# Four reorderings in a ViT-layer kernel: reciprocal root, row normalisation, first low part, tail products

## The reference, cut to what matters

```python
pooled = x.reshape(Bb, Cc, n, K, n, K).sum(axis=(3, 5))      # K = 16, n = 14
h = jnp.einsum('bcij,ce->bije', pooled, channel_weights)     # 196 tokens of 192 for each image
h = h + attention(_layernorm(h))                             # 1 + qk + qk*qk/2, relu, divided by its sum
flat = _layernorm(h)
probs = softmax(flat @ router_w.T)                           # 8 experts
top_w, top_i = jax.lax.top_k(probs, 2)                       # weights normalised to their sum
for e in range(8):
    w_e = jnp.sum(top_w * (top_i == e), axis=-1)[:, None]
    out = out + w_e * (gelu(flat @ w1[e] + b1[e]) @ w2[e] + b2[e])
return h + out
```

## Time and profile before

| | |
|---|---|
| median of 3 runs | 1372.46 us (1367.8 to 1373.46) |
| profiled execution | 1380.3 us, span 1378.5 us |
| granted TensorE clock, mean | 0.939 |
| busy: PE / DVE / ACT / POOL | 1228.3 / 957.9 / 592.9 / 600.3 us |
| DMA | 284.42 MB, mean 206 GB/s |
| steps 0 to 3, alone | to 234 us |
| steps 4 to 15 with three tiles each | 234 to about 1080 us |
| four rounds of whole tiles, three of half tiles | to the end |

### The profile page before, as it was taken

The page is one execution under the profiler, slowest core; times in us unless marked ns, Lnnn a source line. Parts: engine busy times, 40 slices in busy tenths (PEclk is TensorE's granted clock), DMA queues, the critical chain, the costliest instruction groups (busy, mean ns, idle before and its releaser), DMA issues.

```text
span 1378.5 us, 26907 instructions
## 1 busy us (share of the span) xinstructions
PE 1228.3 (89%) x7299; PEld 1091.9 (79%) x7299; DVE 957.9 (69%) x3405; ACT 592.9 (43%) x1127; POOL 600.3 (44%) x485
## 2 busy tenths in 40 slices
PE   5867765999999899998989999999999989999996
PEld 3756654888888788887878888888888878898885
DVE  6799998787878687878777878787765433333453
ACT  1121222444445444544444444444354544444564
POOL 0103434335453545444546454535464554353433
PEclk9975557999999999999999999999999999999998
DMA  9779886778888778787787778787644555454554
GB/s 357 229 253 358 307 292 222 229 224 237 238 229 225 221 209 246 223 247 208 237 225 240 222 238 232 228 244 212 173 111 84 184 127 102 94 115 88 111 123 110
DMA packets 126552, 284.42 MB, mean 206 GB/s; under 512 B 24820, under 2 KB 70501, under 8 KB 126501
## 3 DMA queue, kind: packets, MB, share of 16 engines
q1 hardware_dynamic: 82762, 241.95, 54.0%
q0 software_dynamic: 43104, 41.25, 17.2%
q10 hardware_dynamic: 634, 0.61, 0.2%
HBM read 228.79 MB, written 54.95 MB: 206 GB/s over the span
## 4 chain that ended last, share of the span: by engine, by line
PE 44%; DVE 21%; DMA 11%; issue 11%; POOL 8%; ACT 5%; ACTq 0%; POOLq 0%; DVEq 0%
PE ps L997 15%; PE ps L966 14%; DVE red L1073 8%; DMA result<-ys,ridx 6%; POOL rows_d L608 5%; DMA rows_d<-rows,sloti 4%; PE ps L806 4%; POOL result L623 3%; DVE stats L1201 2%; PE ps L937 2%; PE ps L938 1%; ACT rows L720 1%; ACT hid L731 1%; DVE topi L1210 1%; PE ps L902 1%
## 5 line engine op out<-in xcount | busy, mean ns | idle before, releaser
L623 POOL DMA_INDIRECT result<-ys,ridx x210 | 334.2, 1591 | 325.8 <-issue 152.5
L997 PE MATMUL ps<-w2a,hid 128*128 x2520 | 456.3, 329 | 1.8 <-ACT hid L731 1.8
L997 PEld LDWEIGHTS ps<-w2a,hid 128*128 128x128 f32 x2520 | 419.5, 192 | 13.6 <-issue 2.6
L608 POOL DMA_INDIRECT rows_d<-rows,sloti x256 | 254.1, 993 | 400.3 <-DMA rows_d<-rows,sloti 146.8
L1073 DVE TENSOR_REDUCE red<-xbuf 128x21 f32<-128x672 f32 x448 | 360.0, 841 | 5.2 <-PE ps L870 2.4
L731 ACT ACTIVATE hid<-ps,b1s 128x512 f32<-128x512 f32 (+1 forms) x344 | 222.4, 653 | 229.8 <-PE ps L966 177.3
L966 PE MATMUL ps<-xh,w1h 128*128 128x512 f32 (+1 forms) x344 | 159.8, 465 | 45.5 <-ACT hid L731 32.2
L1333 DVE TENSOR_TENSOR w1l<-w1r,w1h 128x768 fp32r<-128x768 f32 x114 | 108.0, 952 | 81.6 <-ACT w1h L743 80.9
L966 PE MATMUL ps<-xb,w1h 128*128 128x512 f32 (+1 forms) x344 | 131.8, 383 | 0.0
L966 PE MATMUL ps<-xh,w1l 128*128 128x512 f32 (+1 forms) x344 | 131.5, 382 | 0.0
L966 PE MATMUL ps<-xb,w1l 128*128 128x512 f32 (+1 forms) x344 | 131.5, 382 | 0.0
(11 more groups left out here) (165 smaller groups left out, 1609.6 us busy)
## 6 DMA issues: line engine op xcount, KB each, us to landing
xbuf<-x SPq DMA_DIRECT2D x224, 672.0 KB, 5.9
w1r<-L_ffn_w SPq DMA_DIRECT2D x118, 384.0 KB, 4.6
xr<-rows_d SPq DMA_DIRECT2D x48, 402.0 KB, 3.7
result<-h1s SPq DMA_DIRECT2D x32, 294.0 KB
w2a<-L_ffn_w SPq DMA_DIRECT2D x8, 576.0 KB, 7.9
rows_d<-rows,sloti POOLq DMA_INDIRECT x256
rows_d<-pad SPq DMA_DIRECT2D x9, 402.0 KB, 4.6
result<-ys,ridx POOLq DMA_INDIRECT x210, 5.1
```

The costliest lines, as they stand in the source:

```text
L608: pool.indirect_dma_start(rows_d, bass.IndirectOffsetOnAxis(ap=sloti[:, k * NT + t:k * NT + t + 1], axis=0), rows[:, t, :], None).then_inc ...
L623: pool.indirect_dma_start(out, bass.IndirectOffsetOnAxis(ap=ridx[:, b, n:n + 1], axis=0), ys[:, b, n, :], None, compute_op=ALU.add).then_i ...
L997: last = mm(yout(g, b, n), hid[:, m % 3, cols], w, start=False, stop=m == MC - 1 and n % 2 == 1)
```

## The change

ORDER: R goes from the head of the third list to right behind S10 in the second, with it ahead of two names P and of Z1 on VectorE. In the third list V.0 goes from ahead of M1 to behind M2, and V.1 from ahead of M2 to behind W0. TensorE's and GpSimd's own order in ORDER stay as they are. LAST: G2 goes ahead of two names P. G1's Z goes from GpSimd to VectorE. TAIL_ORDER: N2 goes ahead of M5 in each tile; in the second list N3, N4 and N5 of the tile before go ahead of M0, M1 and M2, X0, N0, M3 and X1 go ahead of the row numbers and the row load (`<I B`), and W1 and Z1 behind M5.

```diff
--- before.py
+++ after.py
@@ -161,17 +161,17 @@
 ORDER = [
     """S1 M2 S2 P P L J P N0 N1 N2 X0 M3 W0 X1 S3 N3 P Z0 P P M4 S4 B P M5 W1 P P Z1 P P P Y N4 S5 N5""".split(),
     """M0 M1 M2 S6.0 P S6.1 N0 N1 X0 S6.2 P <I M3 X1 N2 P N3 W0 P S6.3 S7.0 <F <A S7.1 Z0 P P S8.0 L B M4 S8.1 P S8.2 M5 J P S8.3
-       S10 W1 P Z1 P""".split(),
-    """M0 R P <N4 <N5 <Y V.0 S11 M1 V.1 M2 S9 <I W0 V.2 N0 P X0 Z0 V.3 M3 N1 N2 P X1 W1 M4
+       S10 R P W1 Z1 P""".split(),
+    """M0 P <N4 <N5 <Y M1 M2 V.0 S11 S9 <I W0 V.1 V.2 N0 P X0 Z0 V.3 M3 N1 N2 P X1 W1 M4
        I P L B Z1 P P M5 <F Q0 Q1 Q2 Q3 <A""".split(),
     """M0 <Y <N3 <N4 <N5 <J M1 <F <A""".split(),
 ]
 LAST = """S3 P P P P P P P P P P S4 S5 P P P G0 G4 S6.0 S6.1 S6.2 S6.3 S7.0 P S7.1 P P G5 G1 P S8.0 S8.1 S8.2 S8.3 S10
-    R V.0 S11 V.1 V.2 S9 V.3 Q0 Q1 Q2 Q3 P P P P P G2 P P G3 P P P P""".split()
+    R V.0 S11 V.1 V.2 S9 V.3 Q0 Q1 Q2 Q3 P P P G2 P P P P G3 P P P P""".split()
 TAIL_ORDER = [
-    """L B J N0 M2 X0 W0 Z0 M3 X1 N1 M4 M5 W1 Z1""".split(),
-    """M0 M1 L J <N2 <Y M2 <N3 <N4 <N5 <I B N0 N1 X0 M3 X1 N2 M4 W0 Z0 W1 Z1 M5 I <F <A N3 N4 N5""".split(),
-    """M0 L B J <Y <F <A M1 M2 X0 W0 Z0 N0 M3 X1 N1 M4 M5 N2 F A N3 N4 I W1 Z1 N5 Y""".split(),
+    """L B J N0 M2 X0 W0 Z0 M3 X1 N1 M4 N2 M5 W1 Z1""".split(),
+    """<N3 M0 <N4 M1 L J <N5 <Y M2 X0 N0 M3 X1 <I B N1 M4 N2 W0 Z0 M5 W1 Z1 I <F <A N3 N4 N5""".split(),
+    """M0 L B J <Y <F <A M1 M2 X0 W0 Z0 N0 M3 X1 N1 M4 N2 M5 F A N3 N4 I W1 Z1 N5 Y""".split(),
     """M0 M1""".split(),
 ]
 PARTS = CHUNKS * HALVES
@@ -630,7 +630,7 @@
                     wait_first(pool, s_h, j * MC + m + 1)
 
             def Z(j, b, q):
-                if at_end[0] or b in LOW_BY_DVE:
+                if at_end[0] or b % 3 in LOW_BY_DVE:
                     return
                 nb = (b + 1) % 3
                 cols = slice(q * FF // 2, (q + 1) * FF // 2)
@@ -640,17 +640,13 @@
                 nc.gpsimd.tensor_tensor(w1l[:, :, cols], w1r[:, nb, q], w1h[:, :, cols].bitcast(F32),
                                         ALU.subtract).then_inc(s_w1l, 1)
 
-            def G1(s):
-                Z(-1, -1, 0)
-                Z(-1, -1, 1)
-
             wait_first(pool, d_pad, 32)
             for n in range(TP):
                 pool.indirect_dma_start(
                     out, bass.IndirectOffsetOnAxis(ap=padi[:, n:n + 1], axis=0),
                     pad[:, n, 0:E], None, compute_op=ALU.add).then_inc(d_add, 16)
 
-            schedule(pool, {"Q": Q, "H": H, "F": F, "A": A, "Z": Z, "G1": G1})
+            schedule(pool, {"Q": Q, "H": H, "F": F, "A": A, "Z": Z})
 
 
         @block.scalar
@@ -1323,7 +1319,7 @@
                                     xb[KB1:128, nb, 0:128 * g].bitcast(F32), ALU.subtract).then_inc(s_xd, 1)
 
             def Z(j, b, q):
-                if not at_end[0] and b not in LOW_BY_DVE:
+                if not at_end[0] and b % 3 not in LOW_BY_DVE:
                     return
                 nb = (b + 1) % 3
                 cols = slice(q * FF // 2, (q + 1) * FF // 2)
@@ -1344,6 +1340,10 @@
                 count_rows(1)
                 L(-2, -2)
                 L(-1, -1)
+
+            def G1(s):
+                Z(-1, -1, 0)
+                Z(-1, -1, 1)
 
             def G2(s):
                 now[:] = [0, -1]
@@ -1385,7 +1385,7 @@
                     P(s, p)
 
             schedule(dve, {"P": P_left, "S1": S1, "S2": S2, "T2": T2, "S6": S6, "S7": S7, "S8": S8, "S10": S10, "R": R,
-                           "S11": S11, "S9": S9, "L": L, "X": X, "I": I, "Z": Z, "G0": G0, "G2": G2},
+                           "S11": S11, "S9": S9, "L": L, "X": X, "I": I, "Z": Z, "G0": G0, "G1": G1, "G2": G2},
                      before_tail=list_ends)
     return nc
```

## The result

| | before | after |
|---|---|---|
| median | 1370.28 us (1367.8 to 1373.46, 4 runs) | 1355.11 us (1352.08 to 1358.53, 4 runs) |
| profiled execution, span | 1380.3, 1378.5 us | 1355.6, 1353.8 us |
| granted TensorE clock, mean | 0.939 | 0.937 |

The ratio is 0.9881, with a 95% interval of 0.985 to 0.9912: faster by 15.2 us in the medians, where 18.0 us and 1354.5 were forecast. That the total fits is partly luck, as the parts will show. The engines do the same work; the page of the changed kernel gives its first part as

The account below looks back on a forecast made before the run. Bounds: VectorE before the middle, engines' or GpSimd's loop in it, VectorE's `<I` wait at the passage, TensorE in the tail. 4.1 + 4.2 + 2.5 + 3.6 + 3.6 = 18.0 us off the 1372.46 median: 1354.5, range 1341 to 1366.

Parts of the forecast that it names:

- G1 to VectorE: Before the middle: without GpSimd's two subtractions VectorE's long `hot` goes, so S1 of step 4 comes 4.1 us sooner.
- R and V in the middle: Middle steps: the 2.4 us gain before TensorE's fourth chunk leaves 1.55 us a step, as M4 then waits for `xl`.
- GpSimd's loop would take most of it back: Middle: eleven steps by 1.55 would be 17 us, but steps where GpSimd has no slack gain nothing.
- going through the ten with GpSimd's loop as read before: Steps 4 to 14: the larger of GpSimd's loop, the way through `<I`, and 67.4 gives 708.2 us, 2.6 gained.
- 4.2 us for the middle: Eleven middle steps: 2.6 us from ten loops and 1.55 from the step after; bounds 0 and 17.
- the slower rival: Middle: closer loads lengthen landings and GpSimd's loop; 1393 us if all loops were like the 74.1 us one; chance 0.04.
- The scatters that wait for a low part: Ahead of the middle: two scatters lengthened beside low parts would cost GpSimd 1.4 us, covered by ScalarE.
- The passage: Between middle and tail: TensorE's 4.11 us stop and the half clock behind it go; 2.5 us gained, bounds 0 and 7.6.
- What is late next is the same wait once more: Passage: `I` waits for adds, then the pick and `xl`, so M4 of the following tile starts about 1123.9, 3.3 us sooner.
- The tail: Tail products ahead: gaps before M2 and N0 go, 3.6 us in wide and 3.6 in half-width iterations; bounds 4 and 8.5.
- Whole rounds: Three wide tail iterations: waits of 0.84 and 0.34 us go, 1.2 us each, 48.3 instead of 49.6 us.
- Half rounds: Three half-width tail iterations: two gaps of 0.62 us ending in a gelu go, 1.2 us each, near 27 us.

Follow-up runs that it names:

- the changed kernel with the hold: Changed kernel, each GpSimd scatter pair from the fourth on waiting for the third pair before it, instead of two waits per step: 1325.05 us, ratio 0.9658 (first chip).
- X0 late: Changed kernel with X0 behind N0 and N1 in the second tail list, instead of ahead of them: 1345.99 us, ratio 0.9525 (third chip).
- the kernel before with the hold: Kernel before, its scatter pairs from the fourth on each waiting for the third pair before: 1577.71 us, ratio 1.123 (second chip); 1571.29 us, 1.1116 (third).

## Why the prediction was right, and where it wasn't

**G1 to VectorE: right.** Forecast 4.1 us, measured 4.1 from S1 of step 3 to S1 of step 4, and 3.5 to 4.1 at S1 of step 4 against the kernels without it. Two low parts at 0.9 us each behind S7, in the idle time of the earlier trace rows, cost nothing that can be seen.

**R and V in the middle: the size of the engines' part right, its yield wrong.** 1.55 us a step was forecast, and 67.4 us for a step that the engines set; 67.2 to 68.2 were found in the steps that don't wait for GpSimd. That GpSimd's loop would take most of it back was right too: the changed kernel with the hold shows it as the bound. The step that failed is "going through the ten with GpSimd's loop as read before". The loops were read from one execution, in which this stretch is 5 and 12 us longer than in two other kernels with the same ORDER, and held fixed. Eleven steps in the profiles of the first chip:

| | old ORDER | new ORDER |
|---|---|---|
| | 781.2, 768.7, 776.0 | 771.8, 769.8 |

The left column alone spreads over 12.5 us, the means of the two differ by 4.5, and ORDER alone didn't gain. So 4.2 us for the middle is neither confirmed nor refuted, and of the 9.4 us in the table of results a good part is the long profile of before. That the landings lengthen as loads move I had named as the slower rival and given 0.04 as a case by itself; as a part of the sum it may have been there, in the wait of 4.57 us above. The scatters that wait for a low part I had weighed ahead of the middle and not in it, where ORDER brings 8 to 13 more of them.

**The passage: one term was two.** The new tail lists are worth 120.9 and 122.5 against 119.2 us with the old ORDER, and 126.1 against 121.1 with the new: 2 to 5 us, where I took 2.5. But ORDER itself adds 2 to 5 us by its longer last loops (119.2 to 121.1, 120.9 to 126.1; one execution each), which I had costed at nothing, and the two cancel. I also named the wrong next stop. "What is late next is the same wait once more" looked at `I` only. X0 had moved ahead of N0 and N1, and the stops ahead of it had gone: the rows that it reads were due 82.7 us behind S1 of step 15 instead of 88.1, 5.4 us sooner, and they hang on the last scatters' landing. The kernel with X0 late shows that both stops lie one behind the other, and that taking one away gives 0.7 us.

**The tail: too small.** Whole rounds gave 1.7 us each, not 1.2. I had added the two idle times (0.84 and 0.34); in starts of matmuls the gaps are 1.16 and 0.67 us where neighbours are 0.2 apart, so 1.4. Where the last 0.3 us stood is open. Half rounds gave 2.3 and 1.8, not 1.2: I read two gaps per round, and the waits above list six kinds with 4.4 us in two rounds, of which 1.8 us are left; the rest of the 4.1 us gained lies in starts further apart without an idle time, which I did not add up. The last half round with the end gave 3.4 us. Measured for the tail: 12.6 us against 7.2.

**The sum.** Prologue 4.1 forecast, about 3.5 measured; tail 7.2, measured 12.6; middle and passage 6.7, measured about zero (15.2 less 3.5 and 12.6). The total came out by errors against each other: 5.4 us too little for the tail, 7.6 too much for middle and passage. These parts mix medians and single profiles, and hold to a few us. That the profiled execution stood 8 us over the median was right to be carried as a difference, not to be gained.

## What to carry over

Where two loops run side by side, work out what the longer one does once the shorter starts its loads earlier: read it in several executions, not in one, and hold it neither fixed nor free. When an order is changed, list what each moved step reads, and ask when that arrives; the stop moves to the next unmet input, and removing one of two stops in line gave 0.7 us of 4. Gaps of pipelined matmuls are counted from start to start, all of them, whoever ends them.

## What the runs showed of the hardware

**The clock after short stops.** In the kernel before, the stop of M3 (2.1 to 2.7 us) is in five of the eleven steps followed by the lower clock. Busy time of the kernel before in two stretches, each behind such a stop (columns as in the earlier trace rows; the last but two is the granted clock, 1.00 and 0.60):

```profile
573.00:578.00 5.00, 4.14 (x24) 3.90 (x25) 3.26 (x13) 5.00 (x11) 1.78 (x2) 1.00 0.67 230
643.70:648.00 4.30, 4.29 (x14) 3.81 (x15) 2.62 (x9) 4.30 (x10) 0.00 (x0) 0.60 0.89 226
```

The first stands behind a stop of 2.66 us and the second behind one of 2.28, so the stop's length doesn't decide it; the kernel with only LAST and G1 has both outcomes behind 2.65 to 2.7 us. With the old ORDER, steps with the dip have 13.0 to 13.4 us from slots to the next S1 and those without 12.2; the change takes the stop and with it the dip. The 0.5 us stops that remain show none.

**The scatter beside a low part.** A scatter that is issued while VectorE runs its low part (two operands in SBUF) takes up to 1.7 us instead of 0.95. One that is issued before the low part starts takes 0.98 us, and the low part its usual 0.96. Both in the kernel with ORDER alone, VectorE's and GpSimd's timelines:

```profile
1001.65 0.94 DVE L1333 TENSOR_TENSOR w1l<-w1r,w1h 128x768 fp32r<-128x768 f32 x1
1001.74 1.68 POOL L608 DMA_INDIRECT rows_d<-rows,sloti  x1 [0.30 <-issue]
...
995.06 0.98 POOL L608 DMA_INDIRECT rows_d<-rows,sloti  x1 [6.01 <-DVE sloti L1259]
995.87 0.96 DVE L1333 TENSOR_TENSOR w1l<-w1r,w1h 128x768 fp32r<-128x768 f32 x1
```

The first scatter ends 0.83 us behind the end of the low part. So do all 30 that begin under one in this kernel, 0.82 to 0.97 us behind it, whenever they began: the scatter waits for the low part to end, which costs it up to 0.8 us. Two more that begin less than 0.1 us ahead of one are held as well (1.80 and 1.83 us). The Trainium skill ("SBUF — State Buffer", on the shared port pair) has a VectorE instruction with two SBUF inputs and a GpSimd instruction that reads SBUF exclude each other; the trace agrees for a GpSimd instruction that comes second.

**Stops that nothing ends, on some chips.** On two of three chips all five runs with the hold lose time in stops of TensorE and ScalarE that end at nothing in the trace, while GpSimd issues indirect DMAs without a pause; in the kernel before with the hold it is 117 us of TensorE's in the mixing products alone, in the changed one, on the third chip, 31 us in the second product's lines. N2 ahead of M5 alone, without the hold, has 27 us of them on the second chip. The Trainium skill ("Runtime: NRT & Kernel Launch", on the mechanics of instruction fetch) says that each engine's sequencer fetches its instructions by a DMA queue of its own, and that a taken branch to a page outside the two that it holds needs that page fetched before it can go on. That would fit stops near the head of the loop, where S1 stands. But the traces speak against it: they record DMA packets of the kind "instruction" (23 on q8 and 28 on q14 in the kernel before with the hold), all of them before 320 us or behind 1110. From 320 to 1110 us, where most of the stops are, that kernel's DMA queues are only these (queue, kind, packets, MB, share):

```profile
q1 hardware_dynamic: 41892, 126.49, 50.7%
q0 software_dynamic: 23328, 22.85, 17.0%
```

So as far as packets are traced, nothing was fetched there, and the cause is open, as is why one chip is free of it. The kernel before is 36 to 44 us slower on these chips and the changed kernel isn't slower on the one where it ran. Whether the same stops are the reason is not shown, since no trace of the kernel before was taken there; the nearest is N2 alone.
